# Values weighed behind the scores, probabilities copied ahead of the norms: one order of TensorE against another in the local layers

## The chip, the cores and the metric

The kernel runs on one core of one Trainium2 chip. The metric is the device time of one execution in microseconds: 4088.11 us, the median of 3 runs (4081.66 to 4088.88). TensorE (PE; PEld is its row of weight loads, which overlap the products), VectorE (DVE), ScalarE (ACT), GpSimd (POOL) and SyncE (SP) each work through a queue of their own in order, and semaphores tie them together.

## The reference, cut to what matters

Eight blocks follow one another on 2048 tokens (8 sequences of 256) of 128 features. The fourth, a stack of six layers of windowed attention with a gated feed-forward, is the one that the change touches.

```python
def attn_layer(x, Wqkv, qs, ksc, Wo):             # 16 heads of 64
    q, k, v = heads(split(x @ Wqkv))
    q, k = l2norm(q) * qs, l2norm(k) * ksc
    q, k = rotate(q, scale), rotate(k, 1 / scale)
    # windows of 32: each query sees its own window and the one before it
    sim = jnp.where(mask, -big, jnp.einsum('bhwie,bhwje->bhwij', bq, bk2) * 8.0)
    return jnp.einsum('bhwij,bhwje->bhwie', softmax(sim), bv2) ... @ Wo

for i in range(6):
    x = attn_layer(shift_tokens(x), ...) + x
    x = ffn_layer(shift_tokens(x), ...) + x      # layernorm, W1, a * gelu(gate), W2
```

## The kernel before, in words

The eight stages run one after another; the stage that matters is `local_stack`. Its 2048 tokens are four groups of 512 (`GROUPS`), the 16 heads eight pairs (`PAIRS`), and the six layers make 24 layer-and-group steps. One **slot** is one pair of heads of one group in one layer, 192 slots in all; k below is the slot's number in its group of eight. The feed-forward of step f runs beside the eight slots that come behind it, cut into pieces that `beside(s, where)` sets at fixed places of a slot: the output projection (64 pairs of loads and products, L2044) at k=1 early, the down projection of the step before (L2075) at k=1 late, residual turns (L2033) at k=2 early and late, the mean (L2050) and variance (L2055) at k=3 and 4, six rounds of the up projection (L2065) at k=5 to 7. The first eight slots have nothing beside them.

Each slot is a pipeline over all engines, and its work for three neighbouring slots is interleaved by hand. TensorE does in slot s, in this order:

1. `score(s)` (L1983, L1994): the mask by a bf16 product into bank 3, then 64 small products on 64x32 tiles (64 rows, 32 columns of the array), four for each pair of windows;
2. `turn_out(s-2)` (L2028): four transposes of the scaled outputs, 128x128, into bank 4;
3. `project_heads(s+2)` (L1953): queries and keys into banks 0 and 1;
4. the early piece of the feed-forward;
5. `turn_heads(s+1, 0)` (L1978): queries, transposed into bank 4;
6. `project_values(s+2)` (L1963): into bank 2 (`V_BANK`);
7. `turn_heads(s+1, 1)` (L1978): keys;
8. `weigh_values(s-1)` (L2015): 64 x 2 records of small products, again on 64x32 tiles, into banks 6 and 7, the values from `v_at` and the shifted copy `v_moved`;
9. `turn_probs(s)` (L2002): the exponentials of slot s, transposed into bank 2;
10. the late piece.

ScalarE does `copy_out(s-2)` (L2187), the squares of the two halves of the new heads with the exponentials between them (L2155, L2178), `copy_queries(s+1)` (L2170), `copy_values(s+2)` (L2159, frees bank 2 and gives the signal `v_used`), `copy_keys(s+1)` (L2174), its own middle piece, `invert_norms(s+2)` (L2164 Ln and L2166 Exp), and `copy_probs(s)` (L2182, gives `pt_copied`). VectorE does the maximum of the scores and their difference to it (L2366, L2367), the rotary products of slot s+2 (L2275, four, each waiting for the squares of its half), the sums of squares (L2287), and last `scale_out(s-1)` (L2349, L2350, two halves), which divides the weighed values by their sums and gives `o_normed`. GpSimd adds the rotary terms (L1924) and scales by the reciprocal norms (L1930). SyncE moves the values by 32 partitions into `v_moved` (signal `v_shifted`) in the slot in which they were copied, two slots ahead of their use.

What ties the steps of the change: `weigh_values(s)` waits for the probabilities' copy (`pt_copied`, s + 4 with three given ahead), for the moved values, and for `o_normed` at 2 s, which says that `scale_out(s-1)` has read banks 6 and 7. `turn_probs(s)` waits for the exponentials and for `v_used` at s + 3: the values of slot s+2 must have left bank 2. `turn_out(s)` waits for `o_normed` of its own slot. `o_scaled` has one buffer.

Of the kernel before, what the change touches and what calls it, by code (L numbers as in the profile page):

```python
# [86 lines left out]
def spread(ap, n):  # L87

    return ap.unsqueeze(2).to_broadcast([ap.shape[0], ap.shape[1], n])


def wait_apart(eng, sem, value, passed):

    eng.wait_ge(sem, value)
    eng.sem_inc(passed, 1)
# [1654 lines left out]
def local_stack(nc, g, d_in):  # L1750
# [13 lines left out]
    with ExitStack() as ctx:  # L1764
# [39 lines left out]
        o_normed, o_turned = sem("o_normed"), sem("o_turned")  # L1804
# [135 lines left out]
        def _(pe):  # L1940
            pe.wait_ge(made, 1)

            def project_heads(s):

                c, l = group_of(s), layer_of(s)
                if pair_of(s) == 0:
                    pe.wait_ge(xs_ready, GROUPS if l == 0 else turns_before(s // PAIRS - GROUPS) + 2)
                    if c == 0:
                        pe.wait_ge(pair_loaded, l * 16 + 16)
                pe.wait_ge(roped, s * 4 + 4)  # L1950
                pe.wait_ge(squared, s * 2 + 2)
                for k in range(TPG):
                    mm = pe.matmul(g.bank[k // 2][:, (k % 2) * 2 * P:(k % 2 + 1) * 2 * P], tile_tokens(s, k),  # L1953
                                   w_layer[:, l % 2, pair_of(s), 0:2 * P], start=True, stop=True)
                    if k % 2:
                        mm.then_inc(qk_psum, 1)
# [24 lines left out]
            def score(s):  # L1981
                pe.wait_ge(z_ready, s + 1)
                pe.matmul(S_BANK[:, :], ident_b[:, :], mask[:, :, :].rearrange("p x k -> p (x k)"),  # L1983
                          start=True, stop=True, skip_group_check=True)
                wait_apart(pe, k_copied, s + 2, pe_passed)
                for b in range(SPG):
                    for x in range(WINDOWS // 2):
                        column = (b * (WINDOWS // 2) + x) * 2 * W
                        for r in range(2):
                            for hh in range(H):  # L1990
                                ch, w = slice(E * hh, E * (hh + 1)), 2 * x + r
                                query = b * T + w * W
                                row = H * W * r + W * hh
                                mm = pe.matmul(S_BANK[row:row + W, column:column + 2 * W], q_rot[ch, s % 2, query:query + W],  # L1994
                                               k_rot[ch, s % 2, b, w * W:(w + 2) * W], start=False, stop=True, skip_group_check=True)
                mm.then_inc(s_ready, 1)
# [8 lines left out]
            def weigh_values(s):  # L2005
                pe.wait_ge(pt_copied, s + 4)
                pe.wait_ge(v_shifted, s * 32 + 32)
                pe.wait_ge(o_normed, 2 * s) if s else None
                for k in range(TPG):
                    for hh in range(H):  # L2010
                        column = (k % 2 * H + hh) * ROW
                        for r in range(2):
                            for v in range(2):
                                keys, row = slice(2 * W * v, 2 * W * (v + 1)), H * W * v + W * r
                                mm = pe.matmul(g.bank[6 + k // 2][row:row + W, column:column + E + 1],  # L2015
                                               pt[keys, k, r, W * hh:W * (hh + 1)],
                                               (v_at if r else v_moved)[keys, TPG * (s % BUFS) + k, hh, 0:E + 1],
                                               start=True, stop=True, skip_group_check=True)
                    if k % 2:
                        mm.then_inc(o_ready, 1)  # L2020

            def turn_out(s):
                pe.wait_ge(o_normed, 2 * s + 2)
                pe.wait_ge(k_copied, min(s + 4, SLOTS + 1))
                pe.wait_ge(o_copied, s) if s == SLOTS - 1 else None
                for k in range(TPG):
                    src = o_scaled[:, H * k:H * (k + 1), :]
                    mm = pe.transpose(QK_BANK[:, k * P:(k + 1) * P], src.rearrange("p h c -> p (h c)"), g.ident[:, :])  # L2028
                mm.then_inc(o_turned, 1)
# [55 lines left out]
            def beside(s, where):  # L2085
                f, before, k = step(s)
                if before is not None and (k, where) == (1, "late"):
                    project_down(before)
                elif before is not None and (k, where) == (2, "early") and before < FFNS - GROUPS:
                    turn_residual(before, 1)  # L2090
                if f is None:
                    return
                if (k, where) == (1, "early"):
                    project_out(f)
                elif (k, where) == (2, "late"):
                    turn_residual(f, 0)
                elif (k, where) == (3, "early"):
                    mean(f)
                elif (k, where) == (4, "early"):
                    variance(f)  # L2100
                elif (k, where) in UP_AT:
                    project_up(f, UP_AT[k, where])
# [8 lines left out]
            turn_heads(0, 1)  # L2111
            for s in range(SLOTS):
                score(s)
                if s >= 2:
                    turn_out(s - 2)
                if s + 2 < SLOTS:
                    project_heads(s + 2)
                beside(s, "early")
                if s + 1 < SLOTS:
                    turn_heads(s + 1, 0)  # L2120
                if s + 2 < SLOTS:
                    project_values(s + 2)
                if s + 1 < SLOTS:
                    turn_heads(s + 1, 1)
                beside(s, "middle")
                if s:
                    weigh_values(s - 1)
                turn_probs(s)
                beside(s, "late")
            for s in range(SLOTS, SLOTS + PAIRS + 3):  # L2130
# [8 lines left out]
        def _(act):  # L2139
# [40 lines left out]
            def copy_probs(s):  # L2180
                act.wait_ge(pt_ready, s + 1)
                ins = act.activation(pt[:, :, :, :].rearrange("p k r q -> p (k r q)"), V_BANK[:, :], ACT.Copy)  # L2182
                ins.then_inc(pt_copied, 1)
# [26 lines left out]
            def beside(s, where):  # L2210
                f, before, k = step(s)
                if before is not None and (k, where) == (1, "second"):
                    gelus(before)
                elif before is not None and (k, where) == (2, "middle") and before < FFNS - GROUPS:
                    copy_residual(before, 1)
                if f is None:
                    return
                if (k, where) == (3, "first"):
                    copy_residual(f, 0)
                elif (k, where) == (3, "last"):  # L2220
                    square_centred(f)
                elif (k, where) == (4, "middle"):
                    invert_deviation(f)
# [11 lines left out]
            for s in range(SLOTS):  # L2235
                beside(s, "first")
                if s >= 2:
                    copy_out(s - 2)
                if s + 2 < SLOTS:
                    square(s + 2, 0)  # L2240
                exponents(s)
                if s + 2 < SLOTS:
                    square(s + 2, 1)
                beside(s, "second")
                if s + 1 < SLOTS:
                    copy_queries(s + 1)
                if s + 2 < SLOTS:
                    copy_values(s + 2)
                if s + 1 < SLOTS:
                    copy_keys(s + 1)  # L2250
                beside(s, "middle")
                if s + 2 < SLOTS:
                    invert_norms(s + 2)
                copy_probs(s)
                beside(s, "last")
            for s in range(SLOTS, SLOTS + PAIRS + 3):
                if s < SLOTS + 2:
# [7 lines left out]
        def _(dve):  # L2265
# [76 lines left out]
                    copy_up(f, UP_AT[k - 1, "late"])  # L2342

            def scale_out(s):
                for half in range(2):
                    blocks = slice(TPG * half, TPG * (half + 1))
                    src = g.bank[6 + half][:, 0:TPG * ROW].rearrange("p (x c) -> p x c", c=ROW)
                    dve.wait_ge(o_ready, 2 * s + half + 1)
                    own.step(dve.reciprocal(over[:, blocks], src[:, :, E]))  # L2349
                    dve.tensor_tensor(o_scaled[:, blocks, :], src[:, :, 0:E], spread(over[:, blocks], E), ALU.mult).then_inc(o_normed, 1)  # L2350
# [193 lines left out]
```

## Time and profile before

| what | value |
|---|---|
| median of 3 runs | 4088.11 us (4081.66 to 4088.88) |
| span of the profiled execution | 4096.1 us, granted clock 0.907 in the mean |
| PE busy | 3535.7 us (86%), 55,448 products |
| PEld busy | 2690.1 us (66%), 55,640 loads |
| DVE busy | 2806.2 us (69%) |
| ACT busy | 1995.0 us (49%) |
| POOL busy | 1465.8 us (36%) |
| first score load of the local layers to the last | 580.1 to 2369.6 us |
| instruction queue q8 | 428 packets, 7.01 MB |

The profiled execution has no time of its own beside its span; the span lies 8 us above the median. The records of matmuls end by a model, so the row of weight loads, which are short and in order, shows best when TensorE issues and when it waits. In the timelines a row is a run of instructions of one line: its start, its length from the first start to the last end, and in brackets the idle time of that engine before it and what ended it, where that is over 0.1 us. Two rows of one engine may overlap by a few hundredths. "Issue" there stands for a wait whose releaser the profile doesn't show.

### The profile page before, as it was taken

How to read it: one execution, taken by the hardware profiler on the slowest of the kernel's cores; microseconds unless marked ns; L12 is line 12 of the kernel's file. 1: busy time of each engine (PE TensorE's matmuls, PEld its weight loads, DVE VectorE, ACT ScalarE, POOL GpSimd, SP SyncE). 2: the span in 40 equal slices, each digit the busy share in tenths (PEclk: the TensorE clock that was granted, in tenths of full speed). 3: DMA queues.
4: the chain of work that ended last, by engine and by line, in shares of the span. 5: the costliest groups of instructions: out<-in, count | busy, mean ns of one | idle time of the engine just before them, and what ended most of it. 6: DMA issues, size and time to landing. Idle time of an engine off the chain costs nothing. (4 is left out here: it accounts for less than half of the span.)

```text
span 4096.1 us, 127849 instructions
## 1 busy us (share of the span) xinstructions
PE 3535.7 (86%) x55448; PEld 2690.1 (66%) x55640; DVE 2806.2 (69%) x5003; ACT 1995.0 (49%) x3765; POOL 1465.8 (36%) x1373
## 2 busy tenths in 40 slices
PE   6676859999999999999999967989998677669998
PEld 2224448888888888888888845767777552236555
DVE  7994568787777787787787746555555258984454
ACT  5452236666666666666666633444444315531222
POOL 2661035455445444454444422222233104650000
PEclk9897879999999999999999976788888678988999
DMA  0000011011011011011111100000000000010000
GB/s 15 0 1 18 1 64 41 26 46 40 26 45 39 26 45 39 27 46 36 28 28 28 28 7 5 6 7 7 8 7 5 8 7 0 1 62 1 0 0 10
DMA packets 55720, 85.23 MB, mean 21 GB/s; under 512 B 13050, under 2 KB 32532, under 8 KB 54036
## 3 DMA queue, kind: packets, MB, share of 16 engines
q1 hardware_dynamic: 55188, 77.36, 6.3%
q8 instruction: 428, 7.01, 0.7%
q14 instruction: 104, 0.85, 0.1%
HBM read 30.87 MB, written 1.05 MB: 8 GB/s over the span
## 5 line engine op out<-in xcount | busy, mean ns | idle before, releaser
L1924 POOL TENSOR_TENSOR local_rot<-local_term 128x512 f32<-128x512 f32 x384 | 480.5, 1273 | 858.8 <-DVE local_term L2275 858.8
L2275 DVE TENSOR_TENSOR local_term<-bank,local_table 128x512 f32<-128x512 f32 x768 | 486.3, 683 | 114.6 <-ACT local_sq L2155 112.8
L1930 POOL TENSOR_TENSOR local_rot<-local_rot,local_inv 128x512 f32<-128x512 f32 x384 | 399.7, 1062 | 66.8 <-ACT local_inv L2166 45.2
L272 POOL TENSOR_TENSOR mamba_hc<-mamba_state,mamba_c_all 128x512 f32<-128x512 f32 x256 | 326.2, 1296 | 252.7 <-DVE mamba_state L496 237.5
L1953 PE MATMUL bank<-local_w_layer,local_xs 128*128 128x256 f32 x1536 | 367.3, 382 | 4.9 <-ACT local_xs L2149 3.5
L1953 PEld LDWEIGHTS bank<-local_w_layer,local_xs 128*128 128x128 f32 x1536 | 278.8, 192 | 36.3 <-ACT local_xs L2149 3.9
L496 DVE TENSOR_TENSOR_SCAN mamba_state<-bank,mamba_dbu 128x512 f32<-128x512 f32 x256 | 298.0, 1204 | 0.0
L333 PE MATMUL bank<-mamba_hc,ident 128*128 128x512 f32 x512 | 266.4, 646 | 24.0 <-DVEq L505 18.3
L798 DVE SCALAR_TENSOR_TENSOR moe_prod<-bank,moe_b,moe_silu 128x512 f32<-128x512 f32 x160 | 120.1, 751 | 243.5 <-ACT moe_silu L778 242.6
L419 ACT ACTIVATE bank<-mamba_dt,mamba_a_neg 128x510 f32<-128x510 f32 x256 | 176.3, 689 | 225.8 <-DVE mamba_state L496 222.8
L733 PEld LDWEIGHTS bank<-moe_w,moe_gated 128*128 128x128 f32 x1568 | 204.1, 196 | 124.0 <-DVE moe_gated L807 78.7
L778 ACT ACTIVATE moe_silu<-bank,moe_b 128x512 f32<-128x512 f32 x164 | 112.0, 687 | 323.7 <-PE bank L747 323.6
L2187 ACT ACTIVATE local_attn<-bank 128x512 f32<-128x512 f32 x192 | 115.0, 599 | 298.7 <-PE bank L2028 298.7
L2155 ACT ACTIVATE local_sq<-bank 128x512 f32<-128x512 f32 x384 | 227.6, 593 | 60.1 <-PE bank L1953 60.1
L1994 PE MATMUL bank<-local_k_rot,local_q_rot 64*32 64x64 f32 x12288 | 217.3, 218 | 37.5 <-issue 8.5
L733 PE MATMUL bank<-moe_w,moe_gated 128*128 128x128 f32 x1568 | 218.6, 284 | 29.1 <-DVE moe_gated L807 26.5
L2287 DVE TENSOR_REDUCE local_sums_q<-local_sq 128x8 f32<-128x512 f32 x384 | 243.4, 675 | 0.0
L1978 PE MATMUL bank<-ident,local_rot 128*128 128x128 f32 x1536 | 235.2, 276 | 5.3 <-ACT local_q_rot L2170 2.8
L1594 DVE SCALAR_TENSOR_TENSOR delta_qkv<-bank,delta_taps_h,delta_qkv 128x510 f32<-128x510 f32 (+2 forms) x288 | 212.3, 743 | 33.6 <-ACT delta_qkv L1441 26.7
L1994 PEld LDWEIGHTS bank<-local_k_rot,local_q_rot 64*32 64x32 f32 x12288 | 182.8, 107 | 79.6 <-issue 79.5
L2366 DVE TENSOR_REDUCE local_most<-bank 128x8 f32<-128x512 f32 x192 | 132.5, 690 | 118.6 <-PE bank L1994 118.6
L2015 PE MATMUL bank<-local_v_at,local_pt 64*32 64x65 f32 x6144 | 212.2, 218 | 0.0
(356 smaller groups left out, 8295.4 us busy)
## 6 DMA issues: line engine op xcount, KB each, us to landing
local_v_moved<-local_v_at SPq DMA_DIRECT2D x192, 198.0 KB
local_w_layer<-a_w_layer_dram SPq DMA_DIRECT2D x6, 1536.0 KB, 7.2
local_v_moved<-local_v_at SPq DMA_DIRECT2D x192, 33.0 KB
moe_w<-f_w_dram SPq DMA_DIRECT2D x3, 2048.0 KB, 17.6
local_w_o<-a_w_o_dram SPq DMA_DIRECT2D x6, 512.0 KB, 3.8
local_w_up<-a_w_up_dram SPq DMA_DIRECT2D x6, 341.0 KB, 4.0
moe_w<-f_w_dram SPq DMA_DIRECT2D x3, 576.0 KB, 5.2
delta_w_h<-g_w_qkv_dram SPq DMA_DIRECT2D x8, 192.0 KB, 2.3
```

The costliest lines, as they stand in the source:

```text
L272: ins = pool.tensor_tensor(hc[:, n % 2, h, :], state[:, n % 2, h, :], c_all[:, n % 2, :], ALU.mult)
L333: mm = pe.matmul(g.bank[4 + h][:, :], g.ident[:, :], hc[:, n % 2, h, :], start=(s == 0), stop=(s == STATES - 1))
L496: dve.tensor_tensor_scan(state[:, b, h, :], decay_bank(n, h)[:, :], dbu[:, b, h, :], 0.0, ALU.mult, ALU.add).then_inc(scanned, 1)
L733: mm = pe.matmul(g.bank[6][:, i * P:(i + 1) * P], gated[:, j % 2, i * P:(i + 1) * P], w2[:, j, :], start=(j == 0 and i == 0), stop=(not bi ...
L1924: pool.tensor_tensor(rot[:, s % 2, :, f, :], here[:, :, f, :], there[:, :, 1 - f, :], ALU.add).then_inc(summed, 1)
L1930: pool.tensor_tensor(one, one, spread(inv[:, s % 2, heads], E), ALU.mult).then_inc(normalized, 1)
L1953: mm = pe.matmul(g.bank[k // 2][:, (k % 2) * 2 * P:(k % 2 + 1) * 2 * P], tile_tokens(s, k), w_layer[:, l % 2, pair_of(s), 0:2 * P], start= ...
L1978: mm = pe.transpose(QK_BANK[:, k * P:(k + 1) * P], src.rearrange("p h f c -> p (h f c)"), g.ident[:, :])
L1994: mm = pe.matmul(S_BANK[row:row + W, column:column + 2 * W], q_rot[ch, s % 2, query:query + W], k_rot[ch, s % 2, b, w * W:(w + 2) * W], st ...
L2155: act.activation(sq[:, b, :], g.bank[b][:, :], ACT.Square).then_inc(squared, 1)
L2275: dve.tensor_tensor(term[:, which, b, :], g.bank[b][:, :], table[:, which, :, :].rearrange("p n c -> p (n c)"), ALU.mult).then_inc(roped, 1)
L2287: ins = dve.tensor_reduce(sums_q[:, 8 * b:8 * b + 8], sq[:, b, :].rearrange("p (x c) -> p x c", c=E), AX.X, ALU.add)
```

## The change

TensorE's step 8, `weigh_values(s-1)`, moves from between the keys' turn and the probabilities' turn to directly behind `score(s)`, ahead of `turn_out(s-2)`. On ScalarE `copy_probs(s)` moves ahead of `invert_norms(s+2)`. VectorE's `scale_out(s)` waits, from slot 1 on, for `o_turned` at s, that is until the outputs of slot s-1 have been read out of the one buffer `o_scaled`.

```diff
             for s in range(SLOTS):
                 score(s)
+                if s:
+                    weigh_values(s - 1)
                 if s >= 2:
                     turn_out(s - 2)
...
                 beside(s, "middle")
-                if s:
-                    weigh_values(s - 1)
                 turn_probs(s)
                 beside(s, "late")
...
                 beside(s, "middle")
+                copy_probs(s)
                 if s + 2 < SLOTS:
                     invert_norms(s + 2)
-                copy_probs(s)
                 beside(s, "last")
...
             def scale_out(s):
+                dve.wait_ge(o_turned, s) if s else None
                 for half in range(2):
```

## Rows read from the trace of the kernel before

**Rows 1.** Windows: stretch, length, busy (count) of PE, PEld, DVE, ACT, POOL; clock, DMA.
```profile
1500.00:1800.00 300.00, 288.98 (x5541) 253.25 (x5571) 232.33 (x438) 191.99 (x366) 146.78 (x128) 1.00 0.13 37
```

**Rows 2.** Waits by total, 590 to 2370 us: total us, times, longest.
```profile
PEld bank L1994 <- issue: 78.2, 209, 1.1
...
PEld bank L2015 <- issue: 32.0, 190, 0.2
PEld bank L2075 <- issue: 25.5, 22, 1.2
```

**Rows 3.** Timeline of PEld, slot 72 (k=0): start, length, line, tile, count.
```profile
1244.74 0.94 PEld L1994 LDWEIGHTS bank<-local_k_rot,local_q_rot 64*32 64x32 f32 x64 [0.42 <-issue]
1245.77 0.42 PEld L2028 LDWEIGHTS bank<-ident,local_o_scaled 128*128 128x128 f32 x4
...
1248.33 0.97 PEld L1963 LDWEIGHTS bank<-local_w_layer,local_xs 128*128 128x128 f32 x8
...
1250.06 0.11 PEld L2015 LDWEIGHTS bank<-local_v_moved,local_pt 64*32 64x32 f32 x2 [0.17 <-issue]
...
1251.11 0.42 PEld L2002 LDWEIGHTS bank<-ident,local_z 128*128 128x128 f32 x4
...
1251.91 0.94 PEld L1994 LDWEIGHTS bank<-local_k_rot,local_q_rot 64*32 64x32 f32 x64 [0.32 <-issue]
```

**Rows 4.** Timeline of PEld in slot 0, which has no values to weigh.
```profile
586.25 1.00 PEld L1963 LDWEIGHTS bank<-local_w_layer,local_xs 128*128 128x128 f32 x8
...
588.19 0.42 PEld L2002 LDWEIGHTS bank<-ident,local_z 128*128 128x128 f32 x4 [0.54 <-issue]
```

**Rows 5.** Timeline of ACT in slot 0.
```profile
587.48 0.60 ACT L2159 ACTIVATE local_v_at<-bank 128x512 f32<-128x512 f32 x1 [0.30 <-PE bank L1963]
```

**Rows 6.** Timelines of ACT and DVE in slot 72 (k=0).
```profile
1247.33 0.60 ACT L2155 ACTIVATE local_sq<-bank 128x512 f32<-128x512 f32 x1 [0.27 <-PE bank L1953]
...
1247.96 2.48 DVE L2275 TENSOR_TENSOR local_term<-bank,local_table 128x512 f32<-128x512 f32 x4 [0.64 <-ACT local_sq L2155]
...
1252.31 0.43 DVE L2350 TENSOR_TENSOR local_o_scaled<-bank,local_over 128x256 f32<-128x256 f32 x1
```

**Rows 7.** Timelines of PEld and DVE in slot 73 (k=1).
```profile
1266.81 0.86 PEld L2075 LDWEIGHTS bank<-local_w_down,local_hid 128*128 128x128 f32 x7 [1.16 <-issue]
...
1266.02 0.68 DVE L2294 TENSOR_TENSOR xn<-xn,bank 128x512 f32<-128x512 f32 x1
```

**Rows 8.** Timelines of PEld and ACT in slot 74 (k=2).
```profile
1274.88 0.42 PEld L1978 LDWEIGHTS bank<-ident,local_rot 128*128 128x128 f32 x4
...
1277.39 0.42 PEld L2033 LDWEIGHTS bank<-ident,xn 128*128 128x128 f32 x4 [0.46 <-issue]
...
1276.69 0.59 ACT L2149 ACTIVATE local_xs<-bank 64x510 f32<-64x510 f32 x1
```

**Rows 9.** Timelines of PEld and DVE in slot 75 (k=3).
```profile
1278.19 0.94 PEld L1994 LDWEIGHTS bank<-local_k_rot,local_q_rot 64*32 64x32 f32 x64 [0.32 <-issue]
...
1286.03 0.94 PEld L1994 LDWEIGHTS bank<-local_k_rot,local_q_rot 64*32 64x32 f32 x64 [0.32 <-issue]
...
1282.62 0.68 DVE L2298 TENSOR_TENSOR local_xc<-local_xs,bank 128x512 f32<-128x512 f32 x1
```

**Rows 10.** Timelines of PEld and ACT in slot 76 (k=4).
```profile
1290.47 0.97 PEld L1963 LDWEIGHTS bank<-local_w_layer,local_xs 128*128 128x128 f32 x8
...
1293.06 0.42 PEld L2002 LDWEIGHTS bank<-ident,local_z 128*128 128x128 f32 x4
...
1291.67 0.60 ACT L2159 ACTIVATE local_v_at<-bank 128x512 f32<-128x512 f32 x1 [0.30 <-PE bank L1963]
...
1293.36 0.63 ACT L2200 ACTIVATE local_rstd<-local_lg 128x512 f32<-128x512 f32 x1
```

**Rows 11.** Timeline of PEld, one score burst that stops on its way (slot 2).
```profile
596.37 0.92 PEld L1994 LDWEIGHTS bank<-local_k_rot,local_q_rot 64*32 64x32 f32 x60 [0.32 <-issue]
597.81 0.14 PEld L1994 LDWEIGHTS bank<-local_k_rot,local_q_rot 64*32 64x32 f32 x4 [0.51 <-issue]
```

## The prediction

> **What bounds the kernel now.** I looked first at the busy times by stretch. In the local layers (590 to 2370 us, 192 slots) TensorE is busy 289 of 300 us at the full granted clock, VectorE 232, ScalarE 192, GpSimd 147 [rows 1]. So the order of TensorE's queue sets the pace, and the question is what little idle time is left and whose it is. The waits by total give it [rows 2]: the weight-load row stands still 0.17 us ahead of each burst of value weights (32.0 over 190), 0.32 to 0.42 ahead of each score burst (the mask), and 1.16 once per layer and group ahead of the down projection (25.5 over 22). Then the timeline of the weight loads in one plain slot, without feed-forward work beside it [rows 3]: scores, outputs turned, heads, values, keys turned, value weights, probabilities turned, next scores, in 1251.91 - 1244.74 = 7.17 us. A slot beside feed-forward work takes 7.8 to 8.7, the one beside the output projection 18. Last I read ScalarE and VectorE in that slot [rows 6], because they hand TensorE its banks back.
>
> **Taken out: one change of tile shape.** Scores and value weights are both 64x32 tiles, all else 128x128. Before the values the load row idles 0.17 us [rows 3], and behind either burst about 0.1 (0.94 of loads, next block 1.03 later). Back to back, one entry and one exit go: scores plus values now cost 1.03 + 0.17 + 1.05 = 2.25, afterwards 0.94 + 0.94 + 0.10 = 1.98, so -0.27 a slot. The trace has no 64x32 burst behind another; if the second start cost a full entry, 0.17 of it would come back, and below zero it can't go, as the loads already follow each other every 15 ns. I take no entry, for the shape stays.
>
> The Trainium skill, "TensorEngine Tiling (Array Packing)", Key Properties, says that a change of tiling mode, not of tile, drains TensorE; the 0.17 and 0.1 agree. By that rule alone the change is a pure gain, the first rival below.
>
> **Put in: a wait that the burst was covering.** Probabilities and new values share bank 2. turn_probs(s) may not write until ScalarE has copied values s+2 out. Now the keys' turn and the value weights lie between, 2.59 us from the first value load to the first load of the probabilities (1293.06 - 1290.47 [rows 10]; 2.78 in the plain slot [rows 3], where the keys' turn itself waits 0.18), and the copy is over long before. Without the burst the chain is bare. Slot 0 has no values to weigh and shows it: 588.19 - 586.25 = 1.94, with 0.54 idle [rows 4], the copy running from 587.48 to 588.08 [rows 5]. In a settled slot the copy starts 1.20, not 1.23, behind the first load (1291.67 - 1290.47 [rows 10]); with 0.60 for the copy and 0.11 to hand over that is 1.91 against 2.59. This stretch shrinks by 0.68 only, while 0.95 is added between scores and turn_out. Net **+0.27 a slot** on TensorE. The saved change of shape is already in it.
>
> **A longer loop through VectorE.** Weighing s-1 writes banks 6 and 7, which scale_out(s-2) must have read. scale_out stands last in VectorE's slot, behind the rotary products and the sums, and these wait for the squares of the heads, which TensorE projects behind turn_out. Before, that loop ran from turn_out to turn_out: 1.56 to the first square (1247.33 - 1245.77), 0.63 to the products, 4.78 to the end of scale_out (1252.31 + 0.43 - 1247.96), about 0.11 to hand over, as from the residual sum to the down projection [rows 7]; 7.08, just under the slot's 7.17 [rows 3, 6]. Now the weighing stands inside it, 1.05 more: **8.13 us from one weighing to the next**, and a shorter slot waits. The new wait of scale_out for o_turned costs nothing: that turn stands right behind the weighing on TensorE, over 4 us before VectorE gets there; layernorm and the next maximum are queued behind it.
>
> **Slot by slot** (number k in its group of eight):
> - k=0, plain: 7.17 becomes 8.13, +0.96.
> - k=1: +0.27 as everywhere, but the down projection now waits for out_added, behind scale_out, behind the late weighing [rows 7]. With the weighing early, VectorE is free when the projection's sum is ready, and 1.19 (the idle 1.16, and the 0.03 by which loads else overlap) goes: -0.92.
> - k=2: the late residual turn waits for ScalarE's second copy of the residual (ends 1277.28), not for TensorE [rows 8]. From the keys' turn to it 2.51 us stay, nothing shrinks there, and the 0.95 comes in full: +0.95. By the code 20 groups have both turns.
> - k=3: the centring adds its 0.60 to VectorE's part of the loop [rows 9], 8.73 against 7.84: +0.89.
> - k=4: ScalarE makes the deviation ahead of the copy of the probabilities [rows 10]. That copy can start at 1293.9, ends near 1294.5 and hands over at 1294.58; weighing could start at 1290.47 + 1.91 + 0.80 + 0.94 = 1294.12. 0.46 on top of 0.27: +0.73.
> - k=5 to 7: a copy of 0.6 in the loop gives 8.73, below the slots' 8.7 + 0.27: +0.81 for three.
>
> The sum is 3.42 a group; 23 groups give 79. The first eight slots have nothing beside them, seven at some +0.8: 5. Three groups have no early residual turn (-2.0), one of them no down projection either (+1.2). **83 us.**
>
> **The exchange on ScalarE.** Probabilities now come back ahead of the reciprocal norms. Without it the weighing would wait for the sums, Ln and Exp too. The norms come at most one copy (0.6 us, [rows 5]) later, and GpSimd, which scales with them, is then still at its own additions; 147 of 300 busy [rows 1] says that it has room. I count nothing; without this cover it is 0.6 in the slots where GpSimd is last.
>
> **Fetching instructions.** Some 18 of 209 waits before scores fall inside a burst [rows 2]; the burst at 596.37 stops for 0.51 after 60 loads [rows 11]. TensorE's stream comes in 428 packets of 16 KB, one per some 260 of its 111,088 instructions (the table of the profile), and weighing, probabilities and scores use up as many in about 2.8 us. Scores and weighing together are 256 in 1.9. Packet ends fall anywhere, so I expect more such stops, partly under the loop's waits: between -13 (all gone) and +27, and I take +3.
>
> The Trainium skill, "Runtime: NRT & Kernel Launch", Instruction fetch mechanics, has this fetch hidden behind the pace of issue; the 0.51 contradicts it. By that page this term is nought and the sum 83.
>
> **The sum.** 83 + 3 = 86 us on the profiled execution's span of 4096.1, that is 4182. The span lies 8 us above the median of the three runs shown, 4088.1; on that the forecast is **4174**.
>
> **Rivals.**
> 1. *Only the change of shape and the wait at the down projection count; it gets faster.* If probabilities waited for their bank less than the drain saved (the point is an idle time of 0.3 instead of slot 0's 0.54) and VectorE had scale_out done in time: 191 x 0.27 + 22 x 1.19 = 78 us less, 4010. For it: the idle times of [rows 2]. Against it: slot 0 [rows 4], and 7.08 of 7.17 already used by the loop. 6%.
> 2. *The bank wait comes, the loop doesn't bind* (VectorE catches up over several slots, as k=1 gives it time): 191 x 0.27 + 20 x 0.68 - 22 x 1.19 = 39 more, 4127. Against it: only k=1 is long, and k=2 to 7 have copies of their own. 14%.
> 3. *The second burst pays an entry of its own*: 191 x 0.17 = 32 on top, 4206. 10%.
> 4. *The longer burst outruns its instructions*: the upper end, 24 on top, or more if a late packet delays the next: 4198 to 4215. 10%.
> 5. *The change is hidden*: weighing is queued early but waits so long for VectorE that it comes where it came before, with the saved waits against the new: 4088. 3%.
>
> **How the numbers follow.** The forecast has 57%, rivals 2 to 4 make 34 more, all slower: 0.91 for slower by over 0.2% (about what a measurement of this kernel can tell from no change), 0.03 within, 0.06 faster. The range takes in rivals 2 to 4 with the bounds of entry and fetch: 4120 to 4216.
>
> **What would show it.** In the profile of the changed kernel: no idle time between the last score load and the first value load in k=6, 0.5 us ahead of the probabilities' turn released by ScalarE's copy of values; idle time ahead of the weighing, released by VectorE's scale_out, in the slots behind k=0 and k=3 and by the copy of probabilities behind k=4; no wait of 1.16 at the down projection; some 1.1 ahead of the residual's late turn in k=2. Plain slots at 8.1 would bear out the loop, at 7.3 rival 2. I am wrong if probabilities start right behind the keys' turn, or if TensorE stays busy 289 in 300.

## The result, and the profile after

The changed kernel takes **4233.03 us** (median of 4 runs, 4231.62 to 4236.95) against 4086.94 for the kernel before in the same comparison (4081.66 to 4088.88): a ratio of **1.036**, with a 95% interval from 1.034 to 1.038. The forecast was 4174, between 4120 and 4216: slower was right, 146 us instead of 86 was not.

The page of the changed kernel gives the span, the busy times and the instruction queue:

```profile
span 4231.9 us, 128232 instructions
...
PE 3567.9 (84%) x55640; PEld 2691.4 (64%) x55640; DVE 2783.7 (66%) x5003; ACT 1994.0 (47%) x3765; POOL 1461.1 (35%) x1373
...
q8 instruction: 428, 7.01, 0.7%
```

The work is the same, down to the 55,640 loads and the 428 packets of instructions; only the time between pieces of it has grown. The same stretch in the local layers as [rows 1]:

```profile
1500.00:1800.00 300.00, 271.72 (x5202) 232.30 (x5191) 210.55 (x402) 172.52 (x332) 134.40 (x118) 0.99 0.12 35
```

TensorE was busy 289 of these 300 us before and is busy 272 now. The granted clock is at its upper level (2.4 GHz) but for two stretches of 3.4 us, which are taken up below. In 300 us TensorE makes 5202 products instead of 5541, and the other engines are busy 8 to 10% less. So TensorE, which set the pace, now waits. The waits by total say for what (590 to 2518 us: total us, times, longest):

```profile
DVE local_term L2275 <- ACT local_sq L2155: 380.0, 184, 5.2
...
PEld bank L2015 <- issue: 104.9, 111, 1.9
...
PEld bank L2002 <- issue: 95.9, 189, 0.5
...
PEld bank L1994 <- issue: 67.6, 190, 0.4
...
PE bank L2015 <- issue: 55.2, 55, 1.7
PE bank L2002 <- ACT local_v_at L2159: 52.1, 157, 0.5
...
PEld bank L2033 <- issue: 22.6, 20, 1.1
...
PEld bank L2015 <- ACT local_pt L2182: 9.3, 23, 0.4
```

Against [rows 2]: the 0.17 us ahead of each value burst (32.0 over 190) is gone, and so is the row of the down projection (25.5 over 22). New are 0.5 ahead of each turn of the probabilities (95.9 over 189), with ScalarE's copy of the values as the releaser on the product row; 1.1 ahead of the residual's late turn; and 105 us in 111 waits at the value weights. That last row holds two different things, and telling them apart decides this case. Some of the 111 waits stand ahead of a burst: TensorE waits for VectorE or ScalarE. The other 55 stand inside a burst, between two loads that wait for no other engine. The product row has the same 55.

Call the second kind a **stop**: two neighbouring loads of one burst of 64x32 tiles that start more than 0.1 us apart (otherwise they start every 15 ns). Summed from the timeline of loads over the whole stage, with the time from the first score load to the start of the last burst of score loads:

| kernel | first to last score burst, us | stops | their time, us | the rest, us |
|---|---|---|---|---|
| before | 1788.6 | 21, all in scores | 13.0 | 1775.6 |
| changed | 1935.3 | 55, all in values | 70.1 | 1865.2 |
| difference | +146.7 | | **+57.1** | **+89.6** |

The two terms make up the measured difference of 146. (The spans differ by only 136, because the profiled execution of before lay 9 us above its median, outside these layers, in code that is the same.) The stops cost 57, where the prediction had 3. The rest, 90, is the order of the work, for which its sum had 83, and one thing more.

That is TensorE's clock. In the kernel before, the granted clock stays at its upper level from 586 us to the end of these layers. In the changed kernel it falls to the lower level (1.2 GHz, 0.50 in the view) five times, for 3.4 us each. One of these stretches and the time ahead of it (stretch, length, busy and count of the five engines, clock, DMA):

```profile
690.00:700.50 10.50, 8.36 (x170) 6.68 (x165) 7.51 (x15) 6.08 (x12) 6.05 (x6) 1.00 0.09 24
700.50:703.90 3.40, 3.40 (x11) 2.86 (x12) 0.10 (x1) 1.33 (x3) 0.00 (x0) 0.50 0.82 252
```

Each of the five begins less than 1 us behind the end of a stop of 1.5 to 1.9 us, in a value burst of k=4 or 5 that had already waited 0.5 to 0.7 ahead of its start. Not every such burst is followed by one; what decides was not tested. With the stops taken out, these five slots are 1.6 to 1.7 us longer than the median slot of their k, 8 us together. So the order itself costs some 81 of the 90 us. The added stops cost some 65, if the clock that falls behind them is put down to them.

First the order. A plain passage from k=5 to k=6 in the changed kernel (timelines of PEld and ACT, columns as in [rows 3]):

```profile
949.69 0.97 PEld L1963 LDWEIGHTS bank<-local_w_layer,local_xs 128*128 128x128 f32 x8
950.64 0.42 PEld L1978 LDWEIGHTS bank<-ident,local_rot 128*128 128x128 f32 x4
951.60 0.42 PEld L2002 LDWEIGHTS bank<-ident,local_z 128*128 128x128 f32 x4 [0.54 <-issue]
...
953.27 0.92 PEld L1994 LDWEIGHTS bank<-local_k_rot,local_q_rot 64*32 64x32 f32 x61 [0.42 <-issue]
954.08 0.10 PEld L2015 LDWEIGHTS bank<-local_v_moved,local_pt 64*32 64x32 f32 x1
...
955.21 0.42 PEld L2028 LDWEIGHTS bank<-ident,local_o_scaled 128*128 128x128 f32 x4
...
950.89 0.60 ACT L2159 ACTIVATE local_v_at<-bank 128x512 f32<-128x512 f32 x1 [0.30 <-PE bank L1963]
```

The first value load starts at 954.08, while the last score loads are still going in, and both bursts take 955.21 - 953.27 = 1.94 us; the prediction had 1.98. Nothing is paid for a second start. The probabilities' turn comes 1.91 us behind the first load of the new values (951.60 - 949.69), after 0.54 idle and 0.11 behind ScalarE's copy (950.89 + 0.60 = 951.49): the 1.91 of the prediction, to the hundredth.

Then the loop through VectorE, in a k=1 slot, which weighs the values of the k=0 slot (timelines of PEld and DVE):

```profile
978.36 0.94 PEld L1994 LDWEIGHTS bank<-local_k_rot,local_q_rot 64*32 64x32 f32 x64 [0.32 <-issue]
980.16 0.14 PEld L2015 LDWEIGHTS bank<-local_v_moved,local_pt 64*32 64x32 f32 x3 [0.87 <-issue]
...
981.99 0.10 PEld L2015 LDWEIGHTS bank<-local_v_moved,local_pt 64*32 64x32 f32 x1 [1.23 <-issue]
...
979.62 0.43 DVE L2351 TENSOR_TENSOR local_o_scaled<-bank,local_over 128x256 f32<-128x256 f32 x1
```

The first two rows with the last are the loop: the scores' loads end at 979.30, the weighing starts at 980.16, and scale_out's second half ended at 979.62 + 0.43 = 980.05, 0.11 before. This wait was forecast. The third row is a stop in the same burst: 1.23 us, with no engine as releaser. This one was not.

### The profile page after: what moved, and what is told of

The parts are those of the page before. It is cut to its first block and busy times, and to the rows that moved or that the text cites. A ratio compares the mean times of both kernels' runs of the same rounds, so it can differ in the third digit from the quotient of the medians.

```text
span 4231.9 us, 128232 instructions
## 1 busy us (share of the span) xinstructions
PE 3567.9 (84%) x55640; PEld 2691.4 (64%) x55640; DVE 2783.7 (66%) x5003; ACT 1994.0 (47%) x3765; POOL 1461.1 (35%) x1373
## 5 line engine op out<-in xcount | busy, mean ns | idle before, releaser
L2015 PE MATMUL bank<-local_v_moved,local_pt 64*32 64x65 f32 x6144 | 230.1, 217 | 58.8 <-DMA local_v_moved<-local_v_at 33.3
L2015 PE MATMUL bank<-local_v_at,local_pt 64*32 64x65 f32 x6144 | 233.1, 218 | 35.3 <-issue 35.3
L2015 PEld LDWEIGHTS bank<-local_v_moved,local_pt 64*32 64x32 f32 x6144 | 192.5, 106 | 74.1 <-issue 64.8
```

## The experiments

Each row of this table is one kernel, with the columns of the table above; the sections behind it say what each was for. The ratio is to the kernel before in the same comparison. The last column counts the stretches of lower clock in the stage; what they cost is part of the rest.

| kernel | ratio (95%) | stops | their time, us | the rest, us | lower clock |
|---|---|---|---|---|---|
| changed | 1.036 (1.034 to 1.038) | 55 | 70.1 | 1865.2 | 5 |
| exchange_only | 1.000 (0.998 to 1.003) | 26 | 17.1 | 1774.7 | 0 |
| weigh_only | 1.043 (1.038 to 1.047) | 61 | 73.4 | 1879.8 | 5 |
| scale_early | 1.028 (1.024 to 1.033) | 54 | 80.9 | 1825.0 | 5 |
| phase_128 | 1.045 (1.041 to 1.050) | 60 | 73.1 | 1869.0 | 5 |
| turn_between | 1.034 (1.030 to 1.038) | 39 | 32.0 | 1893.3 | 0 |
| heads_between | 1.016 (1.012 to 1.020) | 3 | 0.6 | 1864.4 | 0 |
| gap_between | 1.067 (1.064 to 1.070) | 55 | 37.9 | 2020.9 | 4 |
| gap_ahead | 1.053 (1.050 to 1.056) | 66 | 93.1 | 1907.5 | 8 |
| add_first | 0.992 (0.989 to 0.996) | 23 | 14.7 | 1752.0 | 1 |
| add_first_keys | 0.991 (0.988 to 0.994) | 22 | 17.2 | 1741.0 | 0 |

### The two parts apart: exchange_only and weigh_only

exchange_only is the kernel before with ScalarE's exchange alone:

```diff
+                copy_probs(s)
                 if s + 2 < SLOTS:
                     invert_norms(s + 2)
-                copy_probs(s)
```

> Only the exchange on ScalarE: probabilities are copied ahead of the reciprocal norms, everything else as before. If the exchange is free, as the prediction has it: 4087 within 8 us. If the later norms hold GpSimd and through it the next turn of the heads back, up to 0.6 us in each of 192 slots: up to 115 us more.

4088.81 us against 4088.28. The waits of TensorE's load row are those of [rows 2], the 0.17 ahead of each value burst included:

```profile
PEld bank L1994 <- issue: 81.6, 213, 1.1
...
PEld bank L2015 <- issue: 32.0, 190, 0.2
```

The median slot of each k is the same as before to the hundredth, 75.23 us for a group of eight. By itself the exchange is free: 0 in the sum was right.

weigh_only is the changed kernel with the norms ahead of the probabilities again.

> Only the move of the values behind the scores, with the wait of scale_out; the norms stay ahead of the probabilities. If the probabilities' copy is then the late one (behind sums, Ln and Exp, some 0.9 us later in part of the slots): 15 to 30 us more than the change, about 4255, with idle time ahead of the values released by ScalarE's copy of probabilities. If that copy has slack: 4233, as the change.

4259.09 us, 26 more than the changed kernel. Its waits at the value weights:

```profile
PEld bank L2015 <- issue: 66.9, 61, 2.7
...
PEld bank L2015 <- ACT local_pt L2182: 62.9, 79, 1.0
```

With the norms first the weighing waits 63 us for ScalarE's copy of the probabilities, with the exchange 9. What is left of that in the rest of the stage is 1879.8 - 1865.2 = 15 us, and 3 more are stops. So the exchange belongs to the move: alone it changes nothing, and without it the move costs more. The cost of the change is that of the moved weighing.

### Is it the loop through VectorE? scale_early

The changed kernel with VectorE's scale_out(s-1) right behind the difference of the scores, ahead of the rotary products and the sums, so that the weighing's banks come free some microseconds earlier:

```diff
                 beside(s, "second")
+                if s:
+                    scale_out(s - 1)
...
-                if s:
-                    scale_out(s - 1)
```

> The change with VectorE's scale_out(s-1) moved from the end of its slot to right behind the difference of the scores, ahead of the rotary products. The loop from one weighing to the next then no longer runs through the squares. If that loop of 8.1 us holds k=0, 3 (and k=1 at its start): the plain slots come down to about 7.3, some 30 us less than the change, 4203; the stops inside the bursts stay or grow by 10. If the loop doesn't bind, no change: 4233.

4208.62 us against 4090.82; the text expected 4203. Outside the stops the stage takes 1865.2 - 1825.0 = 40 us less. From one weighing to the next the k=0 slot now takes 7.26 us instead of 8.21 and the k=3 slot 8.07 instead of 8.80, and in the median slot of every k but 5 the weighing starts 0.81 behind the scores' start: its waits for VectorE are gone. In k=5 it still starts 1.34 behind them, after ScalarE's copy of the probabilities. So the loop was real and costs about 40 of the 90 us. The stops went the other way, 70.1 to 80.9. What is left at the value weights is stops (52 of the 53 waits without a releaser) and those waits for ScalarE:

```profile
PEld bank L2015 <- issue: 75.2, 53, 2.4
PE bank L2015 <- issue: 66.4, 52, 2.2
...
PEld bank L2015 <- ACT local_pt L2182: 9.4, 23, 0.4
```

### What are the stops? phase_128

If TensorE waits in mid-burst for none of the other engines, the candidate is its own instructions. Counted over all its records in the trace (sequencer records included, and for before the one product per slot that its trace lacks), the 55 stops of the changed kernel lie, as do the 21 of before, at one place of the count modulo 256, within four records. The packets of queue 8 are 16 KB, one per some 260 instructions of TensorE, so I take that place for the end of a packet. A stop in slot 77 of the changed kernel, in the timeline:

```profile
1354.00 0.17 PEld L2015 LDWEIGHTS bank<-local_v_moved,local_pt 64*32 64x32 f32 x4
...
1356.04 0.11 PEld L2015 LDWEIGHTS bank<-local_v_at,local_pt 64*32 64x32 f32 x2 [1.87 <-issue]
```

and the DMA queues at that time (packets, MB, share), first for the 3.6 us from 1349.9 to 1353.5, then from 1353.5 to 1355:

```profile
q1 hardware_dynamic: 187, 0.23, 23.6%
...
q8 instruction: 1, 0.02, 3.6%
...
q1 hardware_dynamic: 5, 0.00, 1.3%
```

No packet of instructions moves in the 3.6 us before; one starts when the burst is about to run dry, and the burst goes on after it. Over all 55 stops the loads go on 2.2 to 2.9 us after the packet's transfer began. To test this rather than fit it, phase_128 puts 128 instructions of no effect ahead of the slot loop of the changed kernel, half a packet:

```diff
             turn_heads(0, 1)
+            for _ in range(128):
+                pe.sem_inc(pe_passed, 1)
             for s in range(SLOTS):
```

> The change with 128 semaphore increments put on TensorE's queue once, ahead of the first slot; nothing else. In the changed kernel 55 bursts of value weights stop for 70 us in all. If the stops are TensorE running into the end of a 16 KB packet of instructions, they fall at the same place of the packet (every 256th instruction) and so in other slots than before, in a like number (40 to 70, 50 to 90 us), total 4233 within 20. If they come from data, a bank or a DMA that lands late, they stay in the same slots.

The increments themselves delay the local layers by 17 us (first score load at 598.7 instead of 581.9; 0.13 each). There are 60 stops instead of 55, 73.1 us instead of 70.1, 59 of them at the same place of the count modulo 256, and **not one of them lies in a slot that had a stop in the changed kernel**. Code and data of every slot are the same in both; only where the packets end has moved. So the stops belong to the place in the stream of instructions, not to the work. The waits, as in the changed kernel:

```profile
PEld bank L2015 <- issue: 107.5, 114, 1.8
...
PE bank L2015 <- issue: 57.0, 57, 1.7
```

It also shows that this other alignment doesn't help. (The median of 4269.66 is 37 above the changed kernel's, more than 17 + 7; the profiled execution, 4254.88 us, was the fastest of four.)

### Taking the bursts apart: turn_between and heads_between

Two versions of the changed kernel with work between the scores and the weighing, so that the small products no longer come in one run of 256 records (64 loads and 64 products each):

```diff
                 score(s)
-                if s:
-                    weigh_values(s - 1)
                 if s >= 2:
                     turn_out(s - 2)
+                if s:
+                    weigh_values(s - 1)
                 if s + 2 < SLOTS:
                     project_heads(s + 2)
```

> The change with turn_out(s-2) put between scores and values on TensorE: the two bursts of small tiles are kept 0.66 us apart by eight instructions, and each slot pays one more change of tile shape, 0.27 us, some 51 in all. If the 75 us over the steady slots are instruction fetch, a packet's worth now takes some 2.5 us instead of 1.9, the stops shrink to 15 to 35 us and the total stays near 4240. If they aren't, the 51 come on top: 4284.

4229.77 us, no different from the changed kernel, but made up otherwise: the stops fall by 38 us to 32.0, and the rest grows by 28, although the clock no longer falls. The four loads and products of turn_out, whose loads take 0.42 us as in [rows 3], with a way out of the small tiles and back into them, more than halve the stops; but turn_out now waits for VectorE:

```profile
PEld bank L2015 <- issue: 59.3, 223, 1.9
...
PEld bank L2028 <- DVE local_o_scaled L2351: 37.1, 56, 0.8
...
PE bank L2015 <- issue: 22.7, 31, 1.7
```

heads_between puts project_heads(s+2), too, ahead of the weighing.

> The change with turn_out(s-2) and project_heads(s+2) put between scores and values: the weighing stays early, but its burst starts some 2 us and 24 instructions behind the scores', and the squares no longer wait behind it. The wait for bank 2 stays, the change of tile shape is paid in full: 0.54 a slot, less 1.19 at k=1, 1.22 at k=2, 0.35 at k=0, some 85 us on 23 groups. If the rest of the 146 us is instruction fetch in the double burst, no more than 10 us of stops are left: 4087 + 85 = 4172, that is 60 below the change. If it isn't: 4230 or more.

4159.61 us (expected 4172). The waits:

```profile
PEld bank L2002 <- issue: 102.0, 189, 0.5
...
PEld bank L2015 <- issue: 63.0, 191, 0.3
...
PEld bank L2028 <- DVE local_o_scaled L2351: 10.2, 23, 0.4
```

The 191 waits of 0.33 at the value weights are one entry into the small tiles per slot; the row of the product engine for stops is gone. **The stops are 0.6 us instead of 70.1, and the time is 73 us lower.** The rest, 1864.4, is that of the changed kernel within 1 us, but in part by chance: there it holds 8 us of lower clock, here 8 more of the order. By the count, some 95 of the 267 packets end inside a value burst in either kernel. They only aren't waited for here.

### How far back does it reach? gap_between and gap_ahead

That a packet ends in a burst isn't enough, then; what ran shortly before counts. I fitted a rule to the stops of the eight traces made so far (before, the change, and six of the experiments above): a packet arrives a fixed time after some record ahead of its end. The best such rule, 2.6 us after the 176th record ahead, gives 13 us for before, 69 for the change, 37 for turn_between and 0.5 for heads_between. A fit of two numbers needs a test on kernels that it hasn't seen. Both of these are the changed kernel with 8 semaphore increments in each slot, one with them between scores and weighing, the other ahead of the scores:

```diff
                 score(s)
                 if s:
+                    for _ in range(8):
+                        pe.sem_inc(pe_passed, 1)
                     weigh_values(s - 1)
```

> The changed kernel with 8 semaphore increments (0.13 us each, 1.06 together) on TensorE's queue between the scores of slot s and the weighing of slot s-1. Theory: a packet of 256 instructions is asked for some way ahead of its end and arrives a fixed time after that. Fitted to the stops of the kernels run so far: 2.6 us after the 176th record ahead of the end; averaged over all 256 places that an end can have, the rule gives 13.4 us of stops for the kernel before (13.0 in its trace), 69 for the change (70.1), 37 with the outputs' turn between the bursts (32.0), 0.5 with the heads between them too (0.6). From the change's own load times with 1.04 us set in here, it gives 25 us of stops inside the value bursts, 45 below the change. Rival: what counts is how many instructions pass in a slot or in how much time, wherever the slow ones stand: then this run and the next lose the same. The time: 1.04 in each of 191 slots, less what the weighing waits already in k=1, 4 and 5 (2.25 a group), some 6.1 a group or 146 us; 4233 + 146 - 45 = 4334 by the theory.

> The same 8 increments, but ahead of the scores, so that scores and values still follow each other without a gap. By the theory an end inside the value burst reaches back past the start of the scores only in its first third, where the wait was short in any case: 68 us of stops, as in the change without increments (69). By the rival it is the same as with the increments between the bursts, whatever that is. The time by the theory: 4233 + 146 - 1 = 4378, some 43 above the run with the increments between.

gap_between, waits at the value weights (these now include 1.1 us of increments ahead of each burst), then gap_ahead:

```profile
PEld bank L2015 <- issue: 206.4, 206, 2.2
```

```profile
PEld bank L2015 <- issue: 87.1, 71, 2.1
...
PE bank L2015 <- issue: 75.5, 62, 1.9
```

The stops are 37.9 us with the increments between the bursts and 93.1 with the same increments ahead of them. The rival, that only the number of instructions or the time of a slot counts, gives the same for both, and falls. So it counts how fast the instructions shortly ahead of a packet's end go out. The rule itself has the direction but not the size: it said 25 and 68, and that the increments ahead would change nothing, where they added 23 us. So the 176 and the 2.6 are no constants to build on, and what sets off the fetch of a packet stays open.

The times went against the expectation: 4358.76 between (4334 expected) and 4302.59 ahead (4378). The part that failed is the cost of the increments. Between the bursts they cost the rest 156 us, near the 146 expected. Ahead of the scores they cost only 42: in k=5 to 7 the median slots take 9.0 to 9.1 us from weighing to weighing, against 8.9 in the changed kernel, so there TensorE was late with earlier work or would have waited anyway; which of the two was not followed up.

### The one part that the change gains, had without it: add_first and add_first_keys

The prediction credited the change with the 1.19 us at the down projection. That wait can be removed in the kernel before with the order of VectorE's queue alone: in the k=1 slots the residual sum goes ahead of scale_out.

```diff
+                first_add = s % PAIRS == 1
+                if first_add:
+                    beside(s, "last")
                 if s:
                     scale_out(s - 1)
-                beside(s, "last")
+                if not first_add:
+                    beside(s, "last")
```

> The kernel before with one exchange on VectorE, in the slots with k=1 alone: the residual sum of the output projection ahead of scale_out, not behind it. If the down projection's wait of 1.16 us is for that sum and nothing is due right behind it: 22 times 1.19, 26 us less than before, 4061. If the gated product or another signal is as late: 4080 to 4087.

4061.98 us against 4090.82, as expected (4061). The median k=1 slot falls from 17.99 to 16.80, by 1.19 exactly; the wait row of the down projection is gone. TensorE's share in the stretch of [rows 1] rises from 289 to 295 of 300:

```profile
1500.00:1800.00 300.00, 295.43 (x5548) 255.07 (x5541) 232.18 (x435) 191.65 (x365) 144.31 (x127) 0.99 0.12 34
```

add_first_keys adds, in the k=2 slots, ScalarE's second copy of the residual ahead of the copy of the keys, for the 0.46 of [rows 8].

> As add_first, and in the slots with k=2 ScalarE copies the residual ahead of the keys. If the late residual turn waits for that copy alone (0.46 us in 20 slots): 9 us less again, 4052. If the keys' copy, now 1.2 us later, holds the next scores up: no less or more than add_first.

4055.17 us, a ratio of 0.991 (0.988 to 0.994; expected 4052): k=2 falls from 8.29 to 7.85. The 7 us to add_first lie within the scatter of its runs (4039.88 to 4068.28); in the traces the stage is 8 us shorter. Both versions are faster than the kernel before and the changed one, and have nothing of the change in them.

## Why the prediction was wrong in size

**What bounds the kernel** was right: the order of TensorE's queue, with 11 idle us in 300. So every new wait had to come out in the end.

**One change of tile shape less** (-0.27 a slot, no second entry): right. 1.94 for both bursts against 1.98 forecast; rival 3, an entry of its own, falls. By "TensorEngine Tiling (Array Packing)", Key Properties, in the Trainium skill a change of mode drains TensorE; the trace agrees both ways, with no gap between two bursts of the same mode and 0.33 a slot where heads_between parts them again.

**The wait for bank 2** (+0.54 idle, net +0.27): right in the trace, 0.54 in each slot. No run takes it away alone, so its share of the 90 us is worked out, not shown.

**The loop through VectorE**: right, and shown by scale_early. Rival 2, that it doesn't bind, falls. The lengths that the prediction gave the slots, against the time from weighing to weighing, in us:

| k | 0 | 1 | 2 | 3 | 4 | 5 | 6 | 7 |
|---|---|---|---|---|---|---|---|---|
| predicted | 8.13 | 17.07 | 9.24 | 8.73 | 8.56 | 8.97 | 8.97 | 8.97 |
| measured (median) | 8.21 | 16.99 | 9.21 | 8.80 | 8.55 | 8.86 | 8.94 | 8.94 |

No slot is off by more than 0.11. The waits have the forecast releasers: in k=4 the weighing waits for scale_out, which ended at 936.13 + 0.42 = 936.55, and in k=5 for the copy of the probabilities. In the changed kernel (timelines of PEld and DVE):

```profile
935.12 0.94 PEld L1994 LDWEIGHTS bank<-local_k_rot,local_q_rot 64*32 64x32 f32 x64 [0.32 <-issue]
936.67 0.14 PEld L2015 LDWEIGHTS bank<-local_v_moved,local_pt 64*32 64x32 f32 x3 [0.61 <-issue]
...
936.13 0.42 DVE L2351 TENSOR_TENSOR local_o_scaled<-bank,local_over 128x256 f32<-128x256 f32 x1
...
945.22 0.11 PEld L2015 LDWEIGHTS bank<-local_v_moved,local_pt 64*32 64x32 f32 x2 [0.41 <-ACT local_pt L2182]
...
994.57 0.41 PEld L2075 LDWEIGHTS bank<-local_w_down,local_hid 128*128 128x128 f32 x3
...
1006.07 0.42 PEld L2033 LDWEIGHTS bank<-ident,xn 128*128 128x128 f32 x4 [1.14 <-issue]
```

The last two rows are the other two steps: the down projection, which now starts without a wait (1.16 in [rows 7]), and the residual's late turn, which waits 1.14 where "some 1.1" was forecast (0.46 in [rows 8]). A group of eight took 3.27 us more by its medians; the prediction had 3.42. Over the stage the order comes to some 81 us, against 83; the other 8 of the 90 are the lower clock.

**The exchange on ScalarE** (0): right, by exchange_only.

**Fetching instructions: this step failed.** It saw the mechanism in [rows 11], saw that scores and weighing together would use up a packet in 1.9 us, and took +3 within -13 to +27. Measured: **+57**. It is rival 4, at more than twice its price. The prediction shows no working for the +3 or its bounds, and three things were wrong in the sizing. I reckoned with whole packets, as if a stop needed 256 fast instructions in a row since the end before. But the ends ahead of the 55 stops lay mostly 4 to 8 us back, with slow work in between; gap_between against gap_ahead shows that the latest part counts. The new order makes that part fast for most ends that fall into a value burst: some 95 of the 267 packets end there, and 55 stop. And the stops are longer than the one of 0.51 that I had in view: 1.27 us each in the mean, against 0.62 for the 21 of before. I also counted on the loop's waits to hide some of them; in the weighing at 980.16 the wait and the stop stand in one burst, one behind the other. And I took the full granted clock for given: the five falls behind stops cost another 8 us, a term that the prediction doesn't have. With 57 and 8 in place of 3 the sum is 148 on the same steps, against 146 measured.

"Runtime: NRT & Kernel Launch", Instruction fetch mechanics, in the Trainium skill has the fetch hidden behind the pace of issue. That holds for heads_between (0.6 us of stops) and not for the changed kernel (70.1) with the same instructions: here the measurement decides.

## What to carry to other kernels

Long runs of very small products can use up TensorE's instructions faster than they come: look for waits inside a burst that have no releaser, count the records up to them modulo 256, and put slower work between two such bursts rather than joining them for a saved change of shape. Look at the granted clock behind such waits, too: here it fell after five of them. When an instruction moves earlier, look for what it covered where it stood (here the copy out of a shared bank) and for the loop that it enters (here scale_out's): each cost more than the 0.27 us that the move saved. A wait at the pacing engine is often cheapest to remove on the engine that causes it: two exchanges on VectorE and ScalarE gave 0.9%, without touching TensorE.

## What the runs showed of the hardware that was not expected

- TensorE stops at one of every 256 of its records when the instructions ahead of it go out fast: 21 times in before, 55 in the change, 60 in phase_128, where they had moved to other slots. The loads go on 2.2 to 2.9 us after the packet's transfer starts, and the transfer starts 0.3 to 1.9 us before the burst runs dry.
- The granted clock fell from 1.00 to 0.50 five times for 3.4 us in the changed kernel, each time within 1 us of the end of a stop of 1.5 to 1.9 us in a burst that had waited 0.5 to 0.7 before; some 1.7 us lost each time. In before, exchange_only, turn_between and heads_between it didn't fall in these layers.
- The same bursts of scores and values lose 70.1 us to stops back to back and 0.6 with the turn of the outputs and the heads between them.
- A semaphore increment on TensorE's queue takes 0.13 us (128 took 17), against 0.015 from one small load to the next. Eight of them a slot cost 156 us between scores and weighing, 42 ahead of the scores.
